# Expert stage of a vision tower: VectorE takes the pieces of the gates' choice behind both products of a step, not between them

## The reference, cut to what matters

```python
logits = jnp.einsum('bsd,de->bse', x, gate_w) + gate_b
probs = jax.nn.softmax(logits, axis=-1)
top_probs, top_idx = jax.lax.top_k(probs, 2)
top_probs = top_probs / jnp.sum(top_probs, axis=-1, keepdims=True)
dispatch = jnp.sum(jax.nn.one_hot(top_idx, n_experts) * top_probs[..., None], axis=-2)
h1 = jnp.einsum('bsd,edh->bseh', x, w1)
h2 = jnp.einsum('bsd,edh->bseh', x, w2)
hidden = jax.nn.silu(h1) * h2
expert_out = jnp.einsum('bseh,eho->bseo', hidden, w3)
return jnp.einsum('bseo,bse->bso', expert_out, dispatch)
```

## Time and profile before

| what | value |
|---|---|
| three runs, median (lowest to highest) | 2323.94 us (2321.23 to 2324.59) |
| the profiled execution: its own time | 2325.76 us |
| its span, first to last instruction | 2323.8 us |
| mean granted TensorE clock over the span | 0.972 |
| TensorE busy over the span | 2159.6 us (93%) |
| VectorE busy | 2062.1 us (89%) |
| ScalarE busy | 1656.8 us (71%) |
| GpSimd busy | 1721.7 us (74%) |

### The profile page before, as it was taken

The page is one execution under the profiler, slowest core; times in us unless marked ns, Lnnn a source line. Parts: engine busy times, 40 slices in busy tenths (PEclk is TensorE's granted clock), DMA queues, the critical chain, the costliest instruction groups (busy, mean ns, idle before and its releaser), DMA issues.

```text
span 2323.8 us, 48577 instructions
## 1 busy us (share of the span) xinstructions
PE 2159.6 (93%) x13383; PEld 1015.1 (44%) x13383; DVE 2062.1 (89%) x2536; ACT 1656.8 (71%) x4555; POOL 1721.7 (74%) x983
## 2 busy tenths in 40 slices
PE   5768999998889999999999999999999999999977
PEld 4543333333334444444444444444444444444456
DVE  6887777779789999999999999999999999999953
ACT  1433333443368989888888888888888888888855
POOL 0233333333478999999999999999999999999923
PEclk8889999999989999999999999999999999999978
DMA  5113333333221222222222222222222222222201
GB/s 156 23 40 73 73 72 74 77 77 71 71 51 49 54 56 56 58 55 54 55 55 58 55 52 55 58 56 56 51 57 56 55 55 53 58 55 54 53 12 31
DMA packets 175625, 135.54 MB, mean 58 GB/s; under 512 B 53902, under 2 KB 157263, under 8 KB 175440
## 3 DMA queue, kind: packets, MB, share of 16 engines
q1 hardware_dynamic: 166042, 118.02, 20.5%
q10 hardware_dynamic: 9532, 16.91, 3.1%
HBM read 10.51 MB, written 4.19 MB: 6 GB/s over the span
## 4 chain that ended last, share of the span: by engine, by line
POOL 55%; PE 8%; DVE 6%; issue 4%; POOLq 1%; ACT 1%; SPq 0%; DMA 0%; ACTq 0%; DVEq 0%
POOL absd L1889 55%; DVE score L1742 4%; PE pp L1058 1%; PE pp L962 1%; PE pp L1049 1%; PE pp L753 1%; PE pp L1067 1%; POOLq L1888 1%; PE pp L899 1%; POOL score L1893 0%; PE pp L950 0%; PE pp L1041 0%; DVE absd L1690 0%; DVE xn L442 0%; PE pp L861 0%
## 5 line engine op out<-in xcount | busy, mean ns | idle before, releaser
L1742 DVE TENSOR_REDUCE score<-pp 128x16 f32<-128x1024 f32 x1280 | 1489.2, 1217 | 58.6 <-PE pp L962 50.0
L1889 POOL TENSOR_TENSOR absd<-absd 128x2560 f32<-128x2560 f32 x635 | 1449.9, 2283 | 67.3 <-ACT absd L1283 25.9
L962 PE MATMUL pp<-blocks,pick 128*128 128x512 f16 x2560 | 771.9, 383 | 22.1 <-DVE score L1742 10.0
L1283 ACT ACTIVATE absd<-pp 128x512 f32<-128x512 f32 x1280 | 695.2, 599 | 117.5 <-PE pp L950 77.2
L950 PE MATMUL pp<-blocks,pick 128*128 128x512 f16 x1280 | 413.6, 383 | 17.0 <-ACT absd L1283 0.7
L1859 POOL TENSOR_TENSOR absd<-absd,yw 128x512 f32<-128x512 f32 x112 | 149.3, 1333 | 291.2 <-DVE yw L1674 291.1
L962 PEld LDWEIGHTS pp<-blocks,pick 128*128 128x128 f16 x2560 | 209.7, 100 | 334.6 <-DVE score L1742 191.1
L1227 ACT ACTIVATE absd<-pp 128x512 f32<-128x512 f32 x256 | 149.6, 597 | 206.4 <-PE pp L804 139.6
L1690 DVE SCALAR_TENSOR_TENSOR absd<-pp,absd 128x512 f32<-128x512 f32 x256 | 171.5, 686 | 74.5 <-ACT absd L1227 60.3
L950 PEld LDWEIGHTS pp<-blocks,pick 128*128 128x128 f16 x1280 | 119.1, 97 | 242.8 <-ACT absd L1283 154.2
L1286 ACT ACTIVATE absd<-pp 128x512 f32<-128x512 f32 x256 | 138.8, 598 | 100.2 <-PE pp L954 100.1
(11 more groups left out here) (245 smaller groups left out, 2610.0 us busy)
## 6 DMA issues: line engine op xcount, KB each, us to landing
blocks<-qk SPq DMA_DIRECT2D x1032, 64.0 KB, 2.0
blocks<-gT SPq DMA_DIRECT2D x128, 128.0 KB
blocks<-gT ACTq DMA_DIRECT2D x128, 128.0 KB
attn<-score SPq DMA_DIRECT2D x256, 64.0 KB, 2.1
xs<-xn SPq DMA_DIRECT2D x66, 32.0 KB, 1.8
big<-in_wrb_t SPq DMA_DIRECT2D x1, 2064.0 KB
big<-in_x_rows SPq DMA_DIRECT2D x4, 512.0 KB, 6.0
token_rows<-big SPq DMA_DIRECT2D x8, 256.0 KB, 3.3
```

Of the source, the lines that this page charges most:

```text
L962: mm = pe.matmul(ps[bank + n], pick[:, unit % 8 + n, :], blocks[:, b, unit // 16, unit // 8 % 2, :], start=True, stop=True)
L1283: nc.scalar.activation(absd[odd][:, 16 * u + 8 * n:16 * u + 8 * n + 8, :], ps[4 + n].rearrange("p (h w) -> p h w", w=D), ACT.Abs).then_inc ...
L1742: dve.tensor_reduce(score[:, odd, b, 16 * d:16 * d + 16], pp[:, bank:bank + 2, :].rearrange("p n (h w) -> p (n h) w", w=D), AX.X, ALU.add, ...
L1889: nc.gpsimd.tensor_tensor(x[:, :, 0:w], x[:, :, 0:w], x[:, :, w:2 * w], ALU.add).then_inc(X["tree"], 1)
```

## The change

In steps 3 to 7 VectorE asked the generator for one piece behind each of the two products. Now it asks for none there, and for two behind the second product, ahead of the weighing. In steps 3 to 6 this moves one piece in each step, the one that stood between the products, behind the second product; the other piece stays where it was. No instruction is added or dropped. In step 7 the generator is already used up, and nothing moves.

```diff
@@ -1689,8 +1689,10 @@
                             dve.wait_ge(C["y_ps"], n - 1)
                         dve.scalar_tensor_tensor(out=hid[:, 2 * (k % 2) + e, :], in0=ps[2 + e], scalar=1.0 / W_SCALE,
                                                  in1=silu[:, e, :], op0=ALU.mult, op1=ALU.mult).then_inc(C["hid"], 1)
-                        if gates is not None and k >= 3:
-                            next(gates, None)
+
+                    if gates is not None and k >= 3:
+                        next(gates, None)
+                        next(gates, None)
                     if not (at == 0 and k == 0):
                         weigh(g if k else g - 1, b if k else 1 - b, (k - 1) % 8, at if k else at - 1)
                     if k == 0 and not final:
```

## The result

The changed kernel takes 2301.55 us in the median of 4 runs (2299.85 to 2303.39), the kernel before 2323.20 beside it. The ratio is 0.9909 with a 95% interval of 0.9894 to 0.9924: 0.9% faster, 21.7 us. The profiled execution took 2303.39 us with a span of 2301.6, 22.2 less than before.

What follows compares the result with a forecast made beforehand. TensorE was taken as the expert stage's bound, waiting for VectorE's late second products. Terms of 16.0 and 6.0 us, together 22.0, took 2323.94 to 2301.9, put a microsecond higher at 2303.0; range 2298 to 2315.

Steps and rivals of the forecast that it cites:

- The bound and the place of the loss: Loop groups: TensorE sets the pace and loses 1.60 us a group at the second expert's L807, all expected back.
- The price of the contended instructions: Moved L1637, L1645, L1650 on VectorE: short price, L1637 at 0.21 us, unless GpSimd's addition is still running; gates ready 1.2 ahead.
- place and contention as two cases: Loop group on VectorE: short price once moved gives 1.60 us, chance 0.56; unchanged long price gives 1.2, chance 0.20.
- The loop term: Ten groups in the loop at 1.60 us each: 16.0 us.
- The term of the five written-out groups: Groups outside the loop: 1.2 us each, an estimate between 0.5 and 1.6, together 6.0 us.
- the room in front of `disp`: Group 13, written out: 0.69 us free between the end of `disp` and L744, counted as gain.
- L807 still waits for VectorE in steps 5 to 7: Sign that the prediction is wrong: TensorE's next up product still held by VectorE in these steps.
- starts some 22 us earlier at an unchanged length: Sign of success: the stage behind the expert stage begins some 22 us earlier and lasts as long.
- VectorE's chain did not become the bound: Rival, pieces keep their long price: 2309.4 us at 1.2 a group, chance 0.20; 2314.5 at 0.69, chance 0.09.
- the gain did not move elsewhere in the loop: Rival: the wait moves to the group's head or later steps, nothing gained, about 2323 us, chance 0.09.
- VectorE stood in front of the second product: Rival: VectorE idles there for the second SiLU, `disp` comes late, slower at 2342 us, chance 0.06.

Runs made afterwards that it cites:

- runs 4 and 5: The changed order in one step alone, against the kernel before: only step 5, 2315.45 us, ratio 0.9970; only step 6, 2317.28 us in one execution.
- Run 1: The kernel before with its order kept, GpSimd's additions cut to 16 of 512 columns: 2307.36 us, 0.9938 of the kernel before.
- run 6: The changed kernel with both pieces of a step behind the weighing, not ahead of it: 2345.96 us, 1.0103 of the kernel before.
- Run 2: The changed kernel with short additions, GpSimd's additions cut to 16 of 512 columns: 2301.40 us, 0.9913 of the kernel before.
- run 8: The changed kernel with ScalarE's first two SiLUs of a group ahead of its gates wait and first DMA issues: 2306.99 us, 0.9935 of the kernel before.
- run 7: The kernel before with its order kept, VectorE's groups 2 to 11 written out instead of looped: 2314.95 us, 0.9970 of the kernel before.

## Why the prediction was right, point by point

**The bound and the place of the loss.** Right in the loop. Steps 5, 6 and the way to L744 take 2.84, 2.85 and 2.83, all of the 1.60 us came back (1.59), and runs 4 and 5 find the single losses where the earlier trace rows had them.

**The price of the contended instructions.** Right in L1645 and L1650, too low in L1637: I took 0.21 there and it is 0.43, as the copy behind the addition contends as well. In front of step 5's weighing there is a gap of 0.23 that I took as nearly nothing. `disp` is therefore 0.90 ahead of L744 and not 1.2, which costs nothing as TensorE is the bound.

**Why the second product was late.** The prediction weighed place and contention as two cases of how much VectorE would gain. Run 1 shows more: contention alone accounted for 1.51 of the 1.60. The change takes most of the contended time out of the reach of the addition, and what is left of it (L1637 and L1650 at 0.4) stands behind the second product, where TensorE doesn't wait for it. Out of TensorE's way alone is not enough: in run 6 no piece stands between the products either, but the pieces stay in reach, and the group is 28.83. The rule of the Trainium skill, SBUF — State Buffer, section "Who interferes with whom", is that a VectorE instruction with two SBUF inputs contends and a reduction doesn't. The trace agrees: L1644 takes 0.21 in the kernel before although it stands within the addition of 451.28 to 452.55, and L1645 right behind it takes 0.75.

**The sum.** The loop term was 16.0 and measured 15.86. The term of the five written-out groups was 6.0 and measured 3.65: 0.55, 1.41, 0.42, 0.96 and 0.31. That is the step that was mis-sized. In 12 to 14 layer-norm pieces stand behind the weighing, and the next first product is late as well. VectorE and TensorE in group 12 of the changed kernel:

```profile
517.16 0.69 DVE L1674 TENSOR_TENSOR yw<-pp,blocks 128x512 f32<-128x512 f32 x1
517.76 1.21 DVE L355 TENSOR_REDUCE stat<-h 128x16 f32<-128x1024 f32 x1
...
518.89 1.28 DVE L1690 SCALAR_TENSOR_TENSOR absd<-pp,absd 128x512 f32<-128x512 f32 x2
...
519.63 0.39 PE L807 MATMUL pp<-x,absd 128*128 128x512 f16 x1 [0.60 <-DVE absd L1690]
```

This L807 is the first expert's, and moving a piece behind the second product does not help it. I had read the room in front of `disp` and not this second wait. By the sign given in the prediction, L807 still waits for VectorE in steps 5 to 7, it fails in these three groups: their steps 6 and 7 still take 3.43 to 4.19 us in the changed kernel. In group 13 VectorE is the bound, busy for 29.05 of 29.86 us, and a change of order can only give back what GpSimd stretched. L1637, L1645 and L1650 went from 0.68, 0.45 and 0.69 to 0.42, 0.22 and 0.22, together 0.96 less, which is what the group gained; another 0.26 that the layer norm's L365 lost came back in front of L1608. So none of the 0.69 of room came back. Run 2 shows how much contention is left: with short additions as well, the five groups give 6.31 and not 3.65.

**The total** came out at 21.7 us for 21 or so forecast, and part of that is luck: the stage gave 19.5 of the 22.0 in the sum. The first L744 came 1.9 us later in the profile after than before (181.12 to 179.25), and the stretch behind the last one was 4.6 us shorter (1719.9 to 1715.3). The change touches neither. In the profiles of this study the latter lies between 1713.4 and 1720.3, and 2.2 apart for one and the same kernel; I count it as difference between executions. Of the 4.6, 4.4 lie behind GpSimd's first long instruction on the distances (128x2560), which starts at 649.76 before and at 632.01 after; from there to the end of the profile it is 1674.0 and 1669.6 us. The sign "starts some 22 us earlier at an unchanged length" was not met: the last L744 came 17.6 us earlier. Why run 1, whose stage from first to last L744 is 1.1 us shorter than the changed kernel's (404.07 to 405.13), is 5.8 us above it in the median stays open: its profile has 1720.3 behind the stage, and no run told whether that belongs to the kernel. All four of its runs are slower than the changed kernel's slowest, so it is hardly chance of one execution.

**The rivals.** VectorE's chain did not become the bound, and the gain did not move elsewhere in the loop. VectorE stood in front of the second product in step 3 alone, for the 0.19 that is in the 1.47 of the pair at 432.85.

## What to carry to other kernels

Small VectorE instructions that read two SBUF tiles don't have a fixed price: look at what GpSimd does at that moment, and place them outside its instructions, whose phase follows from what VectorE hands over. When one engine waits for another in several steps, removing one wait passes part of it on to the next, so count what comes back by the distance between two fixed points of the loop and not by the table of waits. DMA issues in front of the first work of a group are work of that engine too; spread behind the urgent work, one a step and two behind step 1, they cost TensorE nothing in the loop, while three together cost it a microsecond in every second group.

## What the runs showed of the hardware that I had not expected

- The contention doesn't depend on how little VectorE reads (run 6): L1640, 128 x 4 values, took 1.03 us beside GpSimd's addition and 0.15 to 0.16 otherwise.
- GpSimd's plain copy of one tile (0.40 us) holds up L1637 as its two-input additions do; L1637 ended 0.08 behind it.
- GpSimd can be the one that stands. In group 13 of the kernel before its addition at 564.22 takes 2.10 us and not 1.27; a product of two SBUF tiles on VectorE (L369, 128x1024) had started 0.24 before it.
- One DMA issue on ScalarE took 0.61 us where none had gone just before, two in a row 1.3 to 1.9, and three in a row 2.47 or 3.56 in the loop of run 8 and up to 4.33 outside it.
- In VectorE's loop 0.22 us stood between a short instruction that is waited for and a product that has three waits; written out (run 7), it is gone. In the changed kernel a gap of 0.23 stands in front of step 5's weighing instead, once in each of the ten groups.
